# Output projection of a grouped attention in two ring items of nine 512-column products in place of four of 256 columns

## The reference, cut to what matters

```
q = (latents @ Wq.T).reshape(b, q_len, H, HD)        # H = 16, HD = 96
k = (hidden @ Wk.T).reshape(b, s_len, KV, HD)        # KV = 4; hidden = context + latents, 1857 keys
v = (hidden @ Wv.T).reshape(b, s_len, KV, HD)
...
attn = softmax(q @ k.T * scale)                      # per head, all 1857 keys
out = (attn @ v).reshape(b, q_len, H * HD)
return out @ Wo.T                                    # x = x + this
```

## Time and profile before

| | |
|---|---|
| time of 3 runs, median | 1986.28 us (1984.8 to 1987.23) |
| profiled execution: its time / its span | 1983.97 us / 1982.2 us |
| TensorE matmul busy | 1886.7 us (95%) |
| VectorE / ScalarE / GpSimd busy | 53% / 46% / 32% |
| third stage | about from 1014 us to the end |
| granted TensorE clock in the third stage | full speed from 1017 to 1910 us |

### The profile page before, as it was taken

One profiled execution on the slowest core, in us unless ns is written; L12 is line 12 of the kernel. 1 busy time (PEld: TensorE's weight loads), 2 busy tenths in 40 slices (PEclk: granted clock), 3 DMA queues, 4 the chain that ended last, 5 costly groups with the idle time before them and its releaser, 6 DMA issues. The chain is left out here.

```text
span 1982.2 us, 23779 instructions
## 1 busy us (share of the span) xinstructions
PE 1886.7 (95%) x8840; PEld 1348.1 (68%) x8840; DVE 1041.9 (53%) x2013; ACT 907.7 (46%) x1726; POOL 631.1 (32%) x504
## 2 busy tenths in 40 slices
PE   7999997999999999999899999999999999999997
PEld 6999894444556465555677777767777777767763
DVE  3464435676666765666535454464445455554414
ACT  3333331544344344334146566545655466645650
POOL 0000000000000000000037677657766577665760
PEclk9999995999999999999989999999999999999996
DMA  5978953000111020020186543335544145543101
GB/s 182 287 247 254 291 194 98 0 1 17 43 43 60 11 75 22 22 80 30 65 228 142 129 128 104 103 82 130 133 122 123 42 112 140 130 122 92 57 25 42
DMA packets 192953, 208.46 MB, mean 105 GB/s; under 512 B 87425, under 2 KB 157569, under 8 KB 192838
## 3 DMA queue, kind: packets, MB, share of 16 engines
q1 hardware_dynamic: 177124, 188.92, 33.6%
q10 hardware_dynamic: 15714, 18.03, 3.0%
HBM read 128.90 MB, written 77.94 MB: 104 GB/s over the span
## 5 line engine op out<-in xcount | busy, mean ns | idle before, releaser
L1417 POOL TENSOR_TENSOR pl<-pf,ph 128x512 fp32r<-128x512 f32 (+1 forms) x480 | 623.4, 1321 | 284.9 <-ACT pf L1607 283.9
L1604 ACT ACTIVATE ph<-ps 128x512 fp32r<-128x512 f32 (+1 forms) x480 | 288.1, 600 | 381.0 <-PE ps L1504 303.1
L1690 DVE TENSOR_REDUCE pm<-ps 128x1 f32<-128x464 f32 x480 | 299.3, 636 | 193.7 <-PE ps L1435 192.5
L1140 DVE TENSOR_REDUCE pm<-ps 128x1 f32<-128x400 f32 (+3 forms) x544 | 285.6, 573 | 92.0 <-PE ps L987 88.2
L1047 ACT ACTIVATE pr<-ps 128x512 f32<-128x512 f32 (+1 forms) x416 | 219.8, 600 | 197.4 <-PE ps L919 196.5
L1607 ACT ACTIVATE pf<-ps 128x512 f32<-128x512 f32 (+1 forms) x480 | 289.0, 602 | 5.0 <-POOL pl L1417 3.6
L1406 POOL MEMSET vh<- 128x30 f32 x1 | 0.2, 155 | 701.1 <-POOLq L684 701.1
L932 PE MATMUL ps<-pr,cv 128*64 128x512 f32 (+1 forms) x832 | 212.3, 626 | 0.0
L1525 PE MATMUL ps<-pl,vh 128*97 128x512 f32 (+1 forms) x480 | 190.7, 397 | 1.6 <-POOL pl L1417 0.8
L1522 PE MATMUL ps<-ph,vh 128*97 128x512 f32 (+1 forms) x480 | 191.5, 399 | 0.0
L1523 PE MATMUL ps<-ph,vl 128*97 128x512 f32 (+1 forms) x480 | 189.3, 394 | 0.0
(11 more groups left out here) (264 smaller groups left out, 3132.4 us busy)
## 6 DMA issues: line engine op xcount, KB each, us to landing
woT<-wo_turned SPq DMA_DIRECT2D x30, 768.0 KB, 6.1
v_scr<-vst SPq DMA_DIRECT2D x16, 1152.0 KB
cnat<-in_ctx_dram SPq DMA_DIRECT2D x16, 768.0 KB
q_scr<-qst SPq DMA_DIRECT2D x48, 256.0 KB, 2.5
vh<-v_scr SPq DMA_DIRECT2D x15, 672.0 KB
vl<-v_scr SPq DMA_DIRECT2D x15, 672.0 KB
home<-k_scr SPq DMA_DIRECT2D x14, 696.4 KB, 8.7
k_scr<-home SPq DMA_DIRECT2D x24, 384.0 KB, 7.4
```

Of the source, the lines that this page charges most:

```text
L1140: dve.reduce_max(pm[:, j, ch:ch + 1], src[:, 0:(cuts if s < S else next_cuts)[ch][1]], AX)\
L1417: pool.tensor_tensor(pl[0:m, n % 2, cols], pf[0:m, half, :], ph[0:m, n % 2, cols].bitcast(F32), ALU.subtract).then_inc(plo, 1)
L1604: act.activation(ph[0:keys[kt], n % 2, cols], src, ACT.Exp, scale=S1).then_inc(phi, 1)
L1690: ins = dve.reduce_max(pm[:, j, ch:ch + 1], at[:, 0:cuts[ch][1]], AX)
```

## The change

A stacked item now covers all 512 columns of a tile of 128 queries, so that a set has two of them and not four. The list is written so that they take the places of the first and the third item of before; the place of the second and of the fourth is left empty. The four maxima that stood between keep their places.

```diff
     OC = G * HD1 // P
-    OW = D // 2
+    OW = D
     NO = TT * D // OW
...
             for i in range(NO):
-                order += [("stacked", s - 1, i), most[28 + i]]
+                order += [("stacked", s - 1, i), most[28 + 2 * i], None, most[29 + 2 * i]]
             return order
```

## The result

| | before | after |
|---|---|---|
| time, median | 1985.62 us (4 runs, 1984.8 to 1987.23) | 1971.31 us (4 runs, 1968.34 to 1972.85) |
| ratio, 95% interval | 1 | 0.9929 [0.9915, 0.9944] |
| span of the profiled execution | 1982.2 us | 1968.4 us |

The change makes the kernel 14 us faster, 0.7%. The direction was right, the size was not. The whole gain lies in the third stage: from the first DMA of the sums to the last it takes 841.39 us (1069.06 to 1910.45) in the trace, where before it took 855.06 (1069.27 to 1924.33).

A forecast was written before the change was run, and what follows sets the result against it. TensorE, busy 95% of the span, was taken to bound the third stage, with waits behind late DMAs. Products 1.2 us plus the weights' earlier load 2.7 us gave 3.9 us less, 1982.4 us; range 1977.5 to 1989.

The forecast's parts named there:

- What bounds the kernel: Third stage: TensorE, busy 95% of the span; about 1.9 us of a usual set are waits behind late DMAs.
- The products: Output projection on TensorE: eighteen 512-column products replace 36 of 256, saving 0.08 us a set, 1.2 us over fifteen sets.
- VectorE's additions: Four additions of 425 ns become two of 691, 0.32 us a set less on VectorE, worth nothing in time.
- the values behind the longer item: Tile 10's values start 1.03 us later behind the wider projection item; 2.3 us of cover stay, cost nothing.
- The head start: SyncE's load of projection weights, issued 1.70 us earlier, shortens the queue delaying the sums: 0.3 us at nine boundaries, 2.7 us.
- nine places: Boundaries after sets 2 to 4, 6 to 8, 10 to 12, where VectorE waits for the sums and weights are loaded.
- the upper bounds: 1.8 us for the projection products and 9.9 us for the weights' earlier load, 1.10 us at each of nine boundaries.
- More in the queue cost nothing there: After the third set, 512 KB of `x` between weights and keys; that set took 54.94 us, no longer than its neighbours.
- Long before the sums are issued: The 0.56 MB of weights are through within 2 us of the keys' issue; sums are issued 5.59 us after the keys.
- Only the products: Rival: the weights' earlier load is worth nothing, only 1.2 us from wider projection products, 1985.1 us; chance 0.32.
- The sums meet worse company: Rival: the sums' DMA falls among the values' loads, up to 0.95 us more at nine boundaries, 1993.7 us; chance 0.14.

The follow-up runs named there:

- Experiment 9: Kernel before, loads and 256-column items unchanged, but VectorE's and ScalarE's steps that wait for the DMAs of the sums one tile later: 1967.34 us, 0.9917.
- 10: Changed kernel with VectorE's and ScalarE's steps that wait for the DMAs of the sums one tile later: 1967.7 us, 0.9910.
- experiment 4: Changed kernel, but the weights' load waits for the values of tile 11, so it is 4.4 us ahead of the keys as before the change: 1981.75 us, 0.9991.
- experiment 8: Changed kernel, but the values' loads wait until the sums have landed: 1972.21 us, 0.9936.
- experiments 1: Kernel before, its 256-column items directly behind each other in pairs, so the weights' load is issued as early as in the changed kernel: 1972.59 us, 0.9938.
- experiment 7: Changed kernel with the weights' load moved behind the values' loads in the same queue: 1999.85 us, 1.0077.
- experiments 3 and 5: Weights' load waits for the last maximum, 3.5 us ahead of the keys: on the changed kernel 1981.03 us, 0.9977; on the kernel before 1983.03 us, 0.9994.

## Why the prediction was right or wrong

*What bounds the kernel: right.* TensorE, and what keeps it idle are the waits behind the sums. Experiment 9 shows that these waits were worth at least as much as the change: without them the sets of the kernel before are even, at 53.2 us.

*The products: right in kind, too small by a factor of about two.* Forecast 0.08 us a set, 1.2 us in all, with 1.8 as the upper bound. Measured on TensorE, both items of one set:

```profile
1262.79 1.55 PE L1458 MATMUL ps<-woT,o1sh 128*128 128x512 f32 x6
...
1264.88 0.39 PE L1522 MATMUL ps<-ph,vh 128*97 128x512 f32 x1
...
1268.07 1.54 PE L1458 MATMUL ps<-woT,o1sh 128*128 128x512 f32 x6
...
1270.12 0.39 PE L1522 MATMUL ps<-ph,vh 128*97 128x512 f32 x1
```

2.09 + 2.05 = 4.14 us in place of 4.28, so 0.14 a set and 2.1 in all; by the sets of 9 and 10 it is 0.16, or 2.4. Products that follow each other within an item keep a beat of 0.230 us, not 0.233. In time it hardly shows: 0.9991 with an interval over 1 in experiment 4.

*VectorE's additions and the values behind the longer item: right.* The additions take 692 ns, and TensorE waits at none of them.

*The head start: the mechanism was right, its size was the error.* The step that failed reads "I take 0.3 us, nearer the lower bound" for each of nine places, 2.7 us. The trace gives 1.34 us less at these places on average, of which 0.16 are products; what is left, 1.2 us, is four times the 0.3, and 10.6 us in all. Experiment 4 against the changed kernel gives (0.9991 - 0.9929) x 1985 = 12.3 us. Even the sum with the upper bounds, 1975, lies above the measured time. Three readings led to it:

- *The bounds.* The upper bound, 1.10 us, was the difference to the one set with no weights ahead, 53.98 us. Its loads are the same in the changed kernel, and there it takes 53.07 (1069.06 to 1122.13); over the kernels here it lies anywhere from 53.1 to 54.2. One draw from a spread of 1 us was taken for a limit. With 53.1 the bound would have been 2 us a set, and the sum would have reached 1967.
- *"More in the queue cost nothing there."* The set with `x` in the queue was taken as evidence that the length of the queue hardly matters. Among long queues it hardly does: leads of 3.5 and 4.4 us leave the kernel before in the same place. But all its sets with weights ahead lay on that side, and two points there say nothing of what happens when the queue gets short.
- *"Long before the sums are issued."* That the weights still ahead of the keys, some 0.5 MB, are nearly through within 2 us of the keys' issue fits the traces (357 GB/s in these 2 us on average over the six places without `x`, against 113 in the changed kernel). But it was taken to mean that they no longer matter for the sums. They push back the keys, queries and values behind them, and the sums come through only about when what was issued ahead of them is moved (experiment 8).

*The rivals.* "Only the products" is refuted by experiments 1 and 4. "The sums meet worse company" did not come: the inversion is sooner at every place that was forecast to wait. But its kind exists, one DMA further down: experiment 7 is slower by 0.8% for it.

*What stays open.* How long the queue ahead of the sums takes does not simply follow its amount. At the six places without `x`, from the keys' issue to VectorE's step, 2.8 MB take 12.8 us in the changed kernel and 3.3 MB take 13.6 in the kernel before, but the 3.5 MB of experiments 3 and 5 only 13.0. Why, and whether the time falls by a step between leads of 4.4 and 6.0 us, no run here shows. Experiment 8 has the earliest sums of all and no gain, so the last 0.6 us a set of the changed kernel (53.63 on average over the nine places against 53.03) hang on later steps of the chain as well, whose waits grow there; which of them was not tried apart. The three sets with a layer norm take 68.3 us or more in every kernel here and were left as they are.

## What to carry to other kernels

Where a list of items in order also sets when a load is issued, moving an item moves the load; price the load's new place in its queue before the instructions of the item. When several engines stand still in order for a small DMA that lies beside large ones, move the waiting steps to where the DMA has surely landed: one tile later gave some 16 us here without touching a load, no less than clearing the weights out of the way. A load that is through before the small DMA is issued can still delay it, by what it pushed back. And a bound that comes from one instance of a repeated pattern needs the spread of that instance before it is a bound.

## What the runs showed of the hardware that was not expected

The sums' DMA behind the last set but one, in the changed kernel, beside which no loads of keys or values run:

```profile
1865.83 0.94 DVE L1720 RECIPROCAL sums_inverted<-sums 8x128 f32<-8x128 f32 x1 [6.04 <-DMA sums<-o]
```

It was issued at 1864.04, so a row of 1024 numbers on ScalarE's queue takes 1.8 us from issue to use (VectorE's idle time ahead of it is the wait for the DMA's issue), and in the kernels before and after 6 to 8.6 us beside loads of SyncE's queue. The Trainium skill's rule that the engines take turns between queues (DMA: Bandwidth & Descriptors, Queues, rings and completion order) would let such a small DMA past the others' backlog. The traces here do not show that: in experiment 8 the sums, issued 5.6 us after the keys, were there when 2.22 MB had moved, and 2.21 MB stood ahead of them. The measurement decides: a small DMA here takes about as long as what was issued ahead of it on the other queue. By which mechanism, no run here shows.
